# Local self-attention of the fourth block turned round: keys on partitions, maxima from a pass over the tokens, the next steps' work placed between its units

## What is computed

```python
qkv = jnp.roll(h @ w_qkv + b_qkv, -SHIFT, axis=1).reshape(B, nw, WIN, 3, H, D)
q, k, v = qkv[:, :, :, 0], qkv[:, :, :, 1], qkv[:, :, :, 2]
scores = jnp.einsum('bnqhd,bnkhd->bnhqk', q, k) / jnp.sqrt(D)
attn = jax.nn.softmax(scores, axis=-1)
o = jnp.einsum('bnhqk,bnkhd->bnqhd', attn, v)
x = x + (roll_back(o) @ w_so + b_so) * g_msa
h = _ln(x) * (1 + sc_mca) + sh_mca
# then: q = h @ w_q + b_q; scores against 64 context keys; top_k 16; softmax; values
```

## Time and profile before

| | us |
|---|---|
| median of 3 launches | 1738.19 (1736.76 to 1738.68) |
| the profiled launch, its own time | 1735.72 |
| span of the profile | 1733.8 |
| PE busy, share of the span | 1561.1, 90% |
| DVE busy, share of the span | 1092.2, 63% |
| ACT, POOL busy | 818.4 and 416.1 |
| granted clock of TensorE, mean | 0.962 of full |

### The profile page before, as it was taken

One profiled execution on the slowest core, in us unless ns is written; L12 is line 12 of the kernel. 1 busy time (PEld: TensorE's weight loads), 2 busy tenths in 40 slices (PEclk: granted clock), 3 DMA queues, 4 the chain that ended last, 5 costly groups with the idle time before them and its releaser, 6 DMA issues.

```text
span 1733.8 us, 27477 instructions
## 1 busy us (share of the span) xinstructions
PE 1561.1 (90%) x9541; PEld 906.7 (52%) x9541; DVE 1092.2 (63%) x2965; ACT 818.4 (47%) x1283; POOL 416.1 (24%) x418
## 2 busy tenths in 40 slices
PE   3789998999989999877979999899999889987788
PEld 1546565444443756455754556543444466555566
DVE  1474344899826449799437433489991744879953
ACT  1144331388863535425534434138886354442454
POOL 0150003433007025113205000253300702412230
PEclk8899999899999999999999999999999999999999
DMA  9300005422020000000050000452202000000004
GB/s 323 103 1 1 0 1 140 61 39 39 2 74 1 1 1 2 1 2 1 11 161 1 1 0 1 121 80 39 39 2 74 1 1 1 2 1 2 1 1 146
DMA packets 43336, 64.07 MB, mean 37 GB/s; under 512 B 8634, under 2 KB 32061, under 8 KB 42301
## 3 DMA queue, kind: packets, MB, share of 16 engines
q1 hardware_dynamic: 32845, 40.73, 7.2%
q0 software_dynamic: 8448, 14.96, 5.6%
q10 hardware_dynamic: 1904, 6.55, 1.0%
HBM read 47.28 MB, written 2.10 MB: 28 GB/s over the span
## 4 chain that ended last, share of the span: by engine, by line
issue 44%; PE 34%; POOL 12%; DVE 7%; ACT 2%; DMA 0%; POOLq 0%; ACTq 0%; DVEq 0%
PE ps L933 8%; PE ps L945 7%; POOL wkblk L2393 3%; PE ps L452 3%; PE ps L918 3%; PE ps L1035 3%; PE ps L1027 2%; PE ps L1192 2%; PE ps L562 2%; DVE taken L2195 2%; POOL rstd L2289 1%; DVE taken L2207 1%; DVE m L2190 1%; PE ps L570 1%; PE ps L1145 1%
## 5 line engine op out<-in xcount | busy, mean ns | idle before, releaser
L2064 DVE TENSOR_REDUCE mm<-ps 128x1 f32<-128x1024 f32 x256 | 309.8, 1223 | 36.4 <-PE ps L918 29.5
L1491 ACT ACTIVATE pt<-ps 128x512 f32<-128x512 f32 x512 | 277.2, 600 | 63.4 <-PE ps L933 54.6
L2289 POOL TENSOR_TENSOR rstd<-ve,minus_half 128x4 f32<-128x4 f32 x32 | 36.2, 1131 | 774.6 <-DVE ve L1798 774.6
L933 PE MATMUL ps<-qx,kx 64*128 64x512 f32 x512 | 192.5, 454 | 1.2 <-ACT pt L1491 1.0
L918 PE MATMUL ps<-kx,qx 48*128 48x512 f32 x512 | 190.9, 453 | 1.4 <-DVE mm L2064 1.4
L945 PE MATMUL ps<-pt,v 128*32 128x256 f32 x2048 | 161.4, 396 | 0.0
L933 PEld LDWEIGHTS ps<-qx,kx 64*128 64x128 f32 x512 | 80.8, 188 | 97.6 <-ACT pt L1491 92.3
L1954 DVE TENSOR_TENSOR rlo<-ring,rhi 128x512 fp32r<-128x512 f32 x48 | 33.2, 693 | 127.7 <-ACT ring L1442 127.6
L918 PEld LDWEIGHTS ps<-kx,qx 48*128 48x128 f32 x512 | 77.2, 189 | 25.0 <-issue 15.4
L945 PEld LDWEIGHTS ps<-pt,v 128*32 128x32 f32 x2048 | 43.2, 109 | 87.7 <-ACT pt L1491 62.8
L2331 POOL DMA_DIRECT2D qx<-mxT x64 | 32.0, 506 | 211.8 <-ACT mxT L1483 191.3
(11 more groups left out here) (324 smaller groups left out, 3423.3 us busy)
## 6 DMA issues: line engine op xcount, KB each, us to landing
w<-in_L_xcond_e_w_dram SPq DMA_DIRECT2D x9, 512.0 KB, 7.9
w<-in_L_xcond_e_w_dram SPq DMA_DIRECT2D x3, 1536.0 KB, 12.2
wm<-in_L_xcond_W_mlp_dram SPq DMA_DIRECT2D x4, 1024.0 KB, 8.0
qx<-q_hi POOLq DMA_DIRECT2D x64, 64.0 KB, 2.6
kx<-k_hi POOLq DMA_DIRECT2D x64, 64.0 KB, 2.7
w3a<-in_L_xcond_w_m_dram SPq DMA_DIRECT2D x2, 2048.0 KB, 8.5
s_ada<-in_L_xcond_w_ada_dram ACTq DMA_DIRECT2D x1, 2304.0 KB, 14.3
qx<-q_lo POOLq DMA_DIRECT2D x32, 64.0 KB, 2.6
```

The costliest lines, as they stand in the source:

```text
L933: pe.matmul(ps[:, bank, :], kx[r, p % 4, kc * P:(kc + 1) * P], qx[r, p % 4, half * 512:(half + 1) * 512], start=True, stop=True).then_inc( ...
L1491: act.activation(pt[:, u % 8, half * 512:(half + 1) * 512], ps[:, bank, :], ACT.Exp, scale=QK_SCALE).then_inc(st_read, 1)
L2064: return dve.tensor_reduce(mm[:, p % 2, e, t:t + 1], place(), X, ALU.max).then_inc(ring_read, 1)
L2289: pool.tensor_tensor(rstd[:, k, :], ve[:, k, :], minus_half[:, :], ALU.pow).then_inc(rstd_ready, 1)
```

## The change

- `window_tokens`: a pass with the tokens on partitions, for the maxima alone. A unit is two parts, each of two float32 products over strips of 32 rows (strips 0 and 2, then 1 and 3) with 256 columns. A part 1 waits until the same unit's part 0 has ended (`wt_half`). DVE reduces both banks to 8 maxima per token (`window_maximum`, written to mxw). For units above 8 there is one buffer (banks 0 and 1), and part 0 of a unit waits for DVE's maximum of the unit before.
- `window_turn_maxima(k)` transposes the maxima of four windows, ACT copies them (`maxW`).
- `window_scores` now has keys on partitions: 8 products of strips of 32 rows with 128 columns, and 8 more that subtract the maxima inside PSUM. It uses banks 4 to 7, once for all units, and waits for the exponential of the unit before.
- `window_exp` goes from PSUM straight to wprobT. `window_turn`, `window_copy`, DVE's subtraction and POOL's `wkblk` are gone. ACT writes the keys twice, once for each parity of the head (`kp3`, 4 activations of 512 for each half in place of 2).
- Nine units of the token pass stand ahead of the loop, four of them around the second half's linear products; the other seven follow in the loop at distance 9.
- `residual(5, 0, ...)`, its transposes, the norm `ln(6, 0)` and the queries `query(2, 0)` stand between units 9 to 15, `build_keys(2)` at unit 10.
- The second half's projection, addition, statistics and norm stand inside the first tile of the cross attention: on PE behind `top_scores(0)`, on DVE after `mark(0)` and after `next_best(0)`. POOL's `split3(2)` (splitting weights of the last MLP) stands ahead of the units' end, and two `keep_busy` calls of the first tile give way to one of 8.
- Setup: two small products make bk3, the key bias by parity.

```diff
+                def window_tokens(u, part):
+                    t, c = u // KC, u % KC
+                    k, o = t // TB, t % TB * P
+                    bank = 2 * (u % 2) if u < TB * KC else 0
+                    if part == 1:
+                        pe.wait_ge(wt_half, u0 + u + 1)
...
+                    if part == 0 and u > TB * KC:
+                        pe.wait_ge(wt_read, u0 + u)
+                    elif part == 0 and u >= 2:
+                        pe.wait_ge(wt_read, u0 + u - 1)
+                    for r in (part, 2 + part):
+                        rows = slice(32 * r, 32 * r + 32)
+                        ins = pe.matmul(ps[:, bank + r // 2, r % 2 * D:(r % 2 + 1) * D], qT[rows, k, c, o:o + P], kp3[rows, k, :, c, o:o + P], start=True, stop=True)
+                    ins.then_inc(wt_ready if part else wt_half, 1)
...
                 def window_scores(u):
-                    pe.wait_ge(wk_ready, u0 + u + 1)
-                    for half in range(2):
-                        ins = pe.matmul(ps[:, 2 * (u % 2) + half, :], qT[:, t // TB, c, t % TB * P:(t % TB + 1) * P],
-                                        wkblk[:, u % 2, 4 * half:4 * half + 4, :].rearrange("p h s -> p (h s)"), start=True, stop=True)
+                    if u == 0:
+                        pe.wait_ge(v3_ready, b * NB + NB)
+                    else:
+                        pe.wait_ge(wp_exp, u0 + u)
+                    if u % (TB * KC) == 0:
+                        pe.wait_ge(maxW_ready, b * NB + k + 1)
+                    for odd in range(2):
+                        for r in range(4):
+                            rows = slice(32 * r, 32 * r + 32)
+                            pe.matmul(ps[:, 4 + r, odd * P:(odd + 1) * P], kp3[rows, k, odd, c, o:o + P], qT[rows, k, c, o:o + P], start=True, stop=False)
+                        for r in range(4):
+                            rows = slice(32 * r, 32 * r + 32)
+                            ins = pe.matmul(ps[:, 4 + r, odd * P:(odd + 1) * P], minus_max[rows, c, odd * S:odd * S + 1].broadcast_to([32, P]), maxW[rows, k, o:o + P], start=False, stop=True)
...
+                window_tokens(0, 0)
+                window_tokens(1, 0)
+                window_tokens(0, 1)
+                window_tokens(1, 1)
+                pe.wait_ge(v3_ready, b * NB + 1)
+                for m in range(2 * KC):
+                    window_tokens(2 + m, 0)
+                    window_linear(1, m)
+                    window_tokens(2 + m, 1)
+                window_tokens(6, 0)
+                window_tokens(7, 0)
+                window_tokens(6, 1)
+                window_tokens(7, 1)
                 window_v(1)
-                window_turn(0)
+                window_tokens(8, 0)
+                window_turn_maxima(0)
+                window_tokens(8, 1)
                 for u in range(N_UNIT):
-                    if u + 2 < N_UNIT:
-                        window_scores(u + 2)
-                    window_values(u)
-                    if u + 1 < N_UNIT:
-                        window_turn(u + 1)
-                    if u == N_UNIT - 3:
-                        pe.wait_ge(ws_read, u0 + N_UNIT - 1)
-                        residual(5, 0, False, wso, (wo_ready, u0 + N_UNIT // 2), bank=0)
-                residual(5, 0, True, bank=2)
-                residual(5, 1, False, wso, (wo_ready, u0 + N_UNIT))
+                    window_scores(u)
+                    if u + 9 < N_UNIT:
+                        window_tokens(u + 9, 0)
+                    if u:
+                        window_values(u - 1)
+                    if u + 9 < N_UNIT:
+                        window_tokens(u + 9, 1)
+                    if u == 7:
+                        window_turn_maxima(1)
+                    elif u == 9:
+                        residual(5, 0, False, wso, (wo_ready, u0 + N_UNIT // 2), bank=0)
+                    elif u == 11:
+                        residual(5, 0, True, bank=0, whole=True)
+                    elif u == 14:
+                        ln(6, 0, bank=0)
+                query(2, 0, 14, wq3, bank=0)
+                window_values(N_UNIT - 1)
...
-                ln(6, 0)
+                top_scores(0)
+                residual(5, 1, False, wso, (wo_ready, u0 + N_UNIT))
                 residual(5, 1, True)
-                query(2, 0, 14, wq3)
-                top_scores(0)
+                top_scores(1)
+                keep_busy(3, 8)
                 ln(6, 1)
                 query(2, 1, 14, wq3)
-                top_scores(1)
                 for t in range(TB):
-                    top_scores(t + 2)
-                    keep_busy(5, 4)
                     if t:
+                        top_scores(t + 2)
+                        keep_busy(5, 4)
                         top_turn_outputs(t - 1)
-                    keep_busy(5, 10)
+                        keep_busy(5, 10)
                     top_turn(t)
+                    if t == 0:
+                        top_scores(2)
                     top_values(t)
```

```diff
+                def window_exp(u):
+                    act.wait_ge(ws_ready, u0 + u + 1)
+                    if u >= 2:
+                        act.wait_ge(wpv_done, u0 + u - 1)
+                    act.activation(wprobT[:, u % 2, :, :].rearrange("p (r o) q -> p r (o q)", o=2), ps[:, 4:8, 0:2 * P], ACT.Exp, scale=QK_SCALE).then_inc(wp_exp, 1)
...
+                def window_maximum(u):
+                    dve.wait_ge(wt_ready, w0 + u + 1)
+                    dve.tensor_reduce(mxw[:, t, :].rearrange("p (r n) -> p r n", r=4)[:, :, 2 * c:2 * c + 2],
+                                      ps[:, bank:bank + 2, :].rearrange("p a (g o s) -> p (a g) o s", g=2, o=2), X, ALU.max).then_inc(wt_read, 1)
...
                 for u in range(N_UNIT):
-                    if u + 2 < N_UNIT:
-                        window_centre(u + 2)
-                    window_divide(u)
-                link(residual(5, 0, 2))
-                statistics(6, 0)
-                normalise(6, 0)
-                link(residual(5, 1))
-                statistics(6, 1)
-                build_keys(2)
-                normalise(6, 1)
+                    if u:
+                        window_divide(u - 1)
+                    if u + 9 < N_UNIT:
+                        window_maximum(u + 9)
+                    if u == 10:
+                        build_keys(2)
+                    elif u == 11:
+                        link(residual(5, 0, 0))
+                        statistics(6, 0)
+                    elif u == 13:
+                        normalise(6, 0)
+                window_divide(N_UNIT - 1)
...
                     mark(t)
+                    if t == 0:
+                        link(residual(5, 1))
+                        statistics(6, 1)
...
                     next_best(t)
+                    if t == 0:
+                        normalise(6, 1)
```

More of the change, by code:

```diff
@@ L231, in build @@
         wprobT = at("wprobT", [P, 2, HC, P], F32, RF + 32 * K1)
-        wkblk = at("wkblk", [P, 2, HC, P], F32, RF + 40 * K1)
+        maxW = at("maxW", [P, NB, BLK], F32, RF + 42 * K1)
         vw = at("vw", [P, N_VW], F32R, RC2)
@@ L1057, in _, with window_linear @@
                             ln(5, 0, bank=4)
-                def window_queries_keys(k):
-                    for m in range(2 * KC):
-                        linear(4 * k + m, wqkv3, m, hT[:, k], (hT_ready, b * 2 * N_HT + 2 * (12 + k)) if m == 0 else None).then_inc(qk3_done, 1)
-                        if k == 0 and m == 1:
-                            residual(4, 1, True)
+                u0 = b * N_UNIT
+                def window_linear(k, m):
+                    linear(4 * k + m, wqkv3, m, hT[:, k], (hT_ready, b * 2 * N_HT + 2 * (12 + k)) if m == 0 else None).then_inc(qk3_done, 1)
@@ L1079, in window_scores, with window_turn_maxima @@
+                def window_turn_maxima(k):
+                    pe.wait_ge(wt_read, u0 + TB * KC * (k + 1))
+                    for t in range(TB):
+                        ins = pe.transpose(ps[:, 2 - 2 * k, t * P:(t + 1) * P], mxw[:, TB * k + t, :], ident[:, :])
+                    ins.then_inc(wm_turned, 1)
                 def window_scores(u):
                     t, c = u // KC, u % KC
-                    pe.wait_ge(wk_ready, u0 + u + 1)
+                    k, o = t // TB, t % TB * P
@@ L1725, in _ @@
             dve.wait_ge(consts_ld, 13 * 16)
+            dve.wait_ge(set_dve, 2)
+            for odd in range(2):
+                dve.tensor_scalar(bk3[:, odd, :], colT[:, C_BK3:C_BK3 + KC], parity[:, odd:odd + 1], None, ALU.mult)
             dve.wait_ge(ident_ld, 16)
@@ L2385, in _ @@
                 ln(5, (1,))
-                u0 = b * N_UNIT
-                for u in range(N_UNIT):
-                    t, c = u // KC, u % KC
-                    if u % N_UNIT in (0, N_UNIT // 2):
-                        pool.wait_ge(qk3_ready, b * NB + t // TB + 1)
-                    if u >= 2:
```

(8 more changed lines are left out.)

127 lines of the change are left out of this document (57 added, 70 removed).

## The result

| | us |
|---|---|
| changed kernel, median of 5 launches | 1729.8 (1726.3 to 1730.4) |
| kernel before on the same chip, median of 5 | 1738.7 (1736.8 to 1740.8) |
| ratio | 0.9944 [0.9929, 0.9958] |
| profile of the changed kernel: span, mean granted clock | 1728.0, 0.956 (before 1733.8, 0.962) |

The change makes the kernel 9 us faster. 17.1 were forecast, and 1721: the time lies outside the forecast's own range (1716 to 1727) and inside the wide one that took in rivals A and B (1713 to 1734). The changed stage came out as laid out up to the second tile; what of its gain reaches the end was sized wrong. In each profile the whole time can be cut at two kinds of marks: the start of the fourth block (PE's first product `hT,wqkv`, as in the earlier trace rows) and DVE's first MAX8 of a tile. The table gives tile marks from the block's start on.

What follows compares the result with a forecast made beforehand. DVE's start of the tiles was taken to bound the kernel: first tile 12.8 us earlier, second 8.6, so 17.1 over two sequences, 1735.72 to 1718.6, on the median 1721. Own range 1716 to 1727; eight in ten, 1713 to 1734.

Steps and rivals of the forecast that it cites:

- Rival A: Granted clock falls in PE's new idle times; two per sequence on the path lose 5 to 6 us: 1732, chance 0.13.
- Rival B: First tile's tail: tile 0's queries, scores and values reach DVE after 736.2, 3 us per sequence: 1727, chance 0.10.
- signs of being wrong: Part over 0.7, ring at 4.6, DVE waiting for values in second tile, or shift differing between second tile and sequence end.
- What bounds the kernel: In the top-16 attention's tiles DVE alone sets the time, so its start of the first tile (725.52) counts.
- The unit and the ring: Units 1 to 7: circle of part 0 (0.44), values, hand-over, division and maximum through the single token-pass buffer, 4.13 us.
- The token pass ahead of the loop: Stretch from the fourth block's start at 616.33 through linears, token parts and values, with loop entry at 651.1.
- Given back in the first tile: DVE's first tile also takes the second half's addition, statistics and norm: 16.6 for 12.36, leaving 8.6 gained per sequence.
- POOL's contention: DVE's `normalise(5, 1)` took 4.55 while POOL ran `wkblk`, against 1.37 alone; POOL is now idle there, a small gain.
- Changes of form: PE's switches between tilings, 0.09 to 0.2 each; if each cost double, about 3 us less gained per sequence.
- Rival C: Token parts on two strips do not overlap, 0.88 each, deciding from about 0.80: 4 slower per sequence, 1742, chance 0.07.
- slack of 2.7: First tile: PE's work for tile 0 ends at 733.5, DVE wants the values at 736.2; mostly covers a clock fall.
- Rival D: Ring or token pass shorter than priced and gain not given back whole: 10 to 12 per sequence, 1716 or less, chance 0.10.

Runs made afterwards that it cites:

- the last experiment: Changed kernel with POOL's `split3(2)` put back between the first tile's `centre` and the root of the second norm: 1732.56 us in its one launch.
- The filler: Changed kernel with 26 filler products instead of 8 on PE ahead of the second half's norm in the first tile: 1730.74 us, ratio 0.9952.
- the repeated comparison: Kernel before and changed kernel each measured and profiled once more, unedited: 1738.25 us and 1728.47 us, the latter at ratio 0.9941.

## Why the prediction was right, and what was mis-sized

The time fell in the wide range and the mechanisms of the stage are right. That the median stayed inside is in part luck: 8.9 us of 17.1 arrived, and two of the prediction's own signs of being wrong came true, DVE's wait for values in the second tile and a shift that is smaller at the end than there.

- What bounds the kernel is DVE's start of the tiles, and what it has to do up to the second. That was right: the steps behind are 12.66, as before.
- The unit and the ring: 4.25 for 4.13. The part alone took 0.64 for 0.44, the rest is within 0.1 each. With the division out of the circle it became 3.67, which shows it as a circle and not as anybody's load.
- The token pass ahead of the loop: 34.42 for 34.8; unit 7's scores 61.3 after the block's start for 61.6; `top_scores(0)` 93.8 for 92.8; first MAX8 96.99 for 96.4.
- Given back in the first tile: 16.65 for 16.6, second tile 113.65 for 113.0. The gain there is 7.9 where 8.6 was said.
- POOL's contention: the earlier trace rows's 4.55 became 1.38. The Trainium skill (VectorE: DVE Perf Modes, Two Vector instructions with no wait between them) names a second SBUF read interface that GpSimd shares; the last experiment agrees with 2.04 for 0.17.
- Changes of form: the Trainium skill (TensorEngine Tiling (Array Packing), Key Properties) has a drain for each change of tiling mode. The part's 0.20 over its price may be one; it has the size of the earlier trace rows's 0.09 to 0.2, and doubled prices for all of them (3 us) did not show.
- Rival C, two strips not side by side, was wrong: the part stayed at 0.64, under the 0.80 that decides. (Its own terms, 3.1 and 7, add up to 10.1 and not 10.6.)
- Rival B held in part. From the block's start, tile 0's values ended at 121.9 where 117.2 was laid out. The norm's transposes on PE started 1.6 later (the tile itself started 0.6 later), with PE idle for 4.13 ahead of them where 3.4 was said, and the fall stretched transposes and queries by 3.2. DVE wanted the values 1.7 later too, so the slack of 2.7 was overrun by 0.51, with 0.46 behind it: 0.6 to 1.2 per sequence where B said 3. The filler shows it.
- Rival A, falls in the loop of units: there is none in any of the fourteen profiles. Other versions had them in the token pass ahead of the loop, at about 1.6 each: one fall put the first MAX8 1.65 later, two put it 3.25 later. Rival D, a shorter ring: not so, the first MAX8 came 0.6 later than forecast.

The step of the prediction that was mis-sized is the last one, the 17.1 taken as what the end sees: 8.6 at the second tile, twice, as if the unchanged code behind it took the same time; and the second tile's own slack of 2.7, said to cover a fall. The steps by the two profiles: 17.1 forecast, 15.8 at the second tiles, 14.1 at the eighth, 9.7 at the end; the medians say 8.9 and, in the repeated comparison, 10.7. The second tile takes 1.7 more than 12.66 in both sequences together, of which the filler gives back 1.2. The last stretch costs 1.4, by the fall in the seventh tile. The first sequence pays at the same place: from its eighth tile's first MAX8 to PE's last product of the MLP the two profiles after have 78.34 and 79.05, those before 77.24 without that fall and 78.35 with it, 0.9 more in the mean. The other 0.6 of that row lie in a stretch that took 550.5 and 546.8 in two profiles of the changed kernel. The remaining 1.5 ahead of the first fourth block can't be laid to the change: two profiles of the kernel before differ by 4.0 there, and the one on which the forecast was made had the early one (616.33; of the thirteen other profiles of this study eleven lie at 619.5 to 620.7, two at 617.2 and 617.7).

What stays open is why a fall comes where it does. Idle time in front of it is the same with and without a fall: ahead of the seventh tile's transposes it is 3.02 to 3.05 in all 24 sequences without filler there, and 13 of them have no fall and 11 have one. The Trainium skill (TensorE: Matmul & The Clock Gate, Part 1) says that the window in which the chip watches the engine runs freely and doesn't start with the program, so that one kernel can have differing numbers of slow products from run to run; the two profiles of the kernel before agree with that, and nothing here shows it further. Whether shifting the work by some us moves the falls in untouched code is not shown: the kernel before moves them by itself. Both kernels in which one hole alone was filled showed new falls, but in the token pass, ahead of the filler's first product in the launch, so the filler can't be called their cause.

The best kernels here are those with the maximum ahead of the division and no filler in the seventh tile: 1720.0 to 1722.5, 0.988 to 0.990 of before.

## What to carry to other kernels

When an operand buffer is single, write out the circle through it and see which instructions in it don't need to be there: moving DVE's maximum ahead of an unrelated division took 0.58 off each turn and 3.0 us off the stage in a sequence without falls, where the whole change had taken 7.9 at the second tile. Take a second profile of the kernel before ahead of counting small gains, and sum them between marks: in the kernel before the marks inside the stage agreed to 0.2 us and the spans to 5. And in a PE-heavy kernel with idle holes of 3 to 4 us, expect falls of the clock in code that the change doesn't touch to move the time by a few us in either direction.

## What the runs showed of the hardware

- Two products over two strips of 32 rows took 0.64 to the next start by themselves (662.14 to 662.78 above). In the token pass two such parts over all four strips took 0.64 as well. Timeline of PE, after:

```profile
637.10 0.71 PE L1096 MATMUL ps<-kp,qT 32*128 32x256 f32 x8
637.74 1.99 PE L454 MATMUL ps<-hT,wqkv 128*128 128x512 f32 x4
```

- Strips overlap across unlike steps too: a part of the token pass on two strips ran beside the first scores of the next unit (starts at 663.79 and 663.80).
- A TENSOR_SCALAR of 128x4 went from 0.17 to 2.04 beside a POOL subtraction of 2.34: DVE did not slow down in proportion, its instruction ended when POOL's did (727.89 and 727.87).
- A fall of the granted clock to 0.50 cost 2.6 on 3.7 us of products. One fall in the token pass put the first MAX8 about 1.6 later, two put it 3.25 later; the same program had them in one sequence and not in the other.
